# Fused cross-attention and mixture-of-experts layer: later stack loads of the third half, and filler matmuls in front of the first passes

## What is computed

```
x = x + xattn(layernorm(x), ctx)        # x, ctx: 8 x 256 x 512, channels x tokens
    q, k, v = Wq x + bq, Wk c + bk, Wv c + bv      # 16 heads of 16 channels
    p = softmax(q k / sqrt(16));  out = Wo (p v) + bo
x = x + ffn(layernorm(x))               # rows of 512, rmsnorm, router to 8 experts, top 2,
                                        # gated experts 512 -> 256 -> 512, one shared expert
```

## Time and profile before

| | |
|---|---|
| median of 3 runs | 884.27 us (884.0 to 884.33) |
| the profiled execution, its own time | 882.7 us |
| its span in the trace | 880.9 us |
| mean granted TensorE clock over the span | 0.977 of full speed |
| TensorE busy | 827.0 us, 94% |
| VectorE busy | 518.6 us, 59% |
| ScalarE busy | 401.1 us, 46% |
| GpSimd busy | 223.1 us, 25% |
| moved by DMA | 110.45 MB |

### The profile page before, as it was taken

One profiled execution on the slowest core, in us unless ns is written; L12 is line 12 of the kernel. 1 busy time (PEld: TensorE's weight loads), 2 busy tenths in 40 slices (PEclk: granted clock), 3 DMA queues, 4 the chain that ended last, 5 costly groups with the idle time before them and its releaser, 6 DMA issues. The chain is left out here.

```text
span 880.9 us, 11075 instructions
## 1 busy us (share of the span) xinstructions
PE 827.0 (94%) x3641; PEld 376.0 (43%) x3641; DVE 518.6 (59%) x1043; ACT 401.1 (46%) x751; POOL 223.1 (25%) x206
## 2 busy tenths in 40 slices
PE   6889999999999999999999999999999999999991
PEld 2334333334334333343343355443545555555550
DVE  5686788787777777777778755568532222222220
ACT  1104666656667666666676663110323333323220
POOL 4203013213232132132200111000114444444431
PEclk9879999999999999999999999999999999999996
DMA  8876365546546655565551232941625555455542
GB/s 272 187 195 192 88 136 136 134 90 157 127 109 137 148 136 121 103 160 124 115 108 29 84 92 74 389 148 48 249 63 96 90 92 93 90 95 94 95 84 36
DMA packets 47017, 110.45 MB, mean 125 GB/s; under 512 B 11684, under 2 KB 12708, under 8 KB 42724
## 3 DMA queue, kind: packets, MB, share of 16 engines
q1 hardware_dynamic: 35548, 80.23, 36.0%
q0 software_dynamic: 11328, 29.37, 16.2%
q10 hardware_dynamic: 88, 0.16, 0.1%
HBM read 68.44 MB, written 41.16 MB: 124 GB/s over the span
## 5 line engine op out<-in xcount | busy, mean ns | idle before, releaser
L850 DVE TENSOR_REDUCE negmax<-front_ps 128x1 f32<-128x512 f32 x512 | 323.8, 682 | 108.7 <-PE front_ps L702 108.3
L637 ACT ACTIVATE probs<-st_ps 128x512 f32<-128x512 f32 x512 | 280.1, 600 | 187.0 <-PE st_ps L736 186.6
L1289 PE MATMUL big_ps<-w_gu,attn 128*128 x312 | 140.4, 593 | 0.8 <-ACT attn L1138 0.8
L1099 POOL DMA_INDIRECT out<-x_sb,row_i x39 | 61.7, 1583 | 136.0 <-DMA out<-x_sb,row_i 108.5
L736 PE MATMUL st_ps<-stacks 50*128 50x512 f32 x256 | 78.7, 496 | 7.6 <-ACT probs L637 4.4
L1483 DVE TENSOR_TENSOR zeros<-attn,big_ps 128x256 f32<-128x256 f32 x39 | 16.4, 421 | 116.4 <-ACT attn L1157 116.4
L1289 PEld LDWEIGHTS big_ps<-w_gu,attn 128*128 128x128 f32 x312 | 56.2, 190 | 57.0 <-issue 57.0
L736 PE MATMUL st_ps<-q_stack,k_stack 50*128 50x512 f32 x256 | 74.8, 492 | 3.8 <-ACT probs L637 2.7
L702 PE MATMUL front_ps<-stacks 48*128 48x512 f32 x256 | 71.3, 450 | 5.5 <-DMA stacks<-parts_dram 3.0
L374 POOL TENSOR_TENSOR attn<-attn,recip 128x512 f32<-128x512 f32 x15 | 19.2, 1279 | 207.8 <-DMA recip<-rec_dram 207.8
L673 PE MATMUL proj_ps<-early,w_t 128*128 128x512 f32 x128 | 67.2, 647 | 4.7 <-ACT early L590 2.5
(11 more groups left out here) (167 smaller groups left out, 902.0 us busy)
## 6 DMA issues: line engine op xcount, KB each, us to landing
parts_dram<-early SPq DMA_DIRECT2D x32, 512.0 KB, 4.7
stacks<-parts_dram SPq DMA_DIRECT2D x32, 256.0 KB, 5.6
w_gu<-in_gate_up SPq DMA_DIRECT2D x8, 1024.0 KB, 14.4
x_sb<-in_x SPq DMA_DIRECT2D x8, 512.0 KB, 7.4
early<-in_ctx POOLq DMA_DIRECT2D x8, 512.0 KB, 8.2
stacks<-parts_dram SPq DMA_DIRECT2D x32, 128.0 KB, 6.3
k_stack<-parts_dram SPq DMA_DIRECT2D x16, 256.0 KB, 5.0
q_stack<-parts_dram SPq DMA_DIRECT2D x16, 256.0 KB, 5.8
```

Source lines behind the costliest of these rows:

```text
L637: nc.scalar.activation(probs[:, k % 2, u % GH, :], score_bank(UNITS * s + u), ACT.Exp, scale=SCALE).then_inc(exp_done, 1)
L850: nc.vector.tensor_reduce(negmax[:, n % 2, c:c + 1], smax_bank(UNITS * n + u), AX_X, ALU.max, negate=True).then_inc(max_done, 1)
L1099: nc.gpsimd.indirect_dma_start(out_rows, bass.IndirectOffsetOnAxis(ap=row_i[:, k:k + 1], axis=0), y_sb[:, k % RING, :], None, compute_op=A ...
L1289: mm = nc.tensor.matmul(gu_ps[:, :], h_t[:, k % 2, a, :], w_gu[:, bass.ds(expert, 1), a, :], start=(a == 0), stop=(a == DT - 1))
```

## The change

SP puts off the loads of half 2's stacks: the k stack's four transfers go behind the store of the second piece of half 0's maxima rows, the q stack's four behind the loads of that piece. In front of both it waits for `first_loaded`, the arrival of the first piece. `FIRST` is 3, so `FIRST - 1` is half 2. TensorE gets three fillers of 512 columns in front of the first pass of half 0, behind the bias product, and one such filler behind each of the two pairs of first passes of half 1. The definition of `filler` only moves up.

```diff
--- before.py
+++ after.py
@@ -487,9 +487,13 @@
                     for i in range(2):
                         write_part(n, i)
                     for i in range(2):
-                        load_stack(n, i)
+                        if n < FIRST - 1:
+                            load_stack(n, i)
+                sp.wait_ge(first_loaded, 16 * TILES)
                 rows_half_out(sp, 1)
+                load_stack(FIRST - 1, 0)
                 rows_half_in(sp, 1, rows_loaded[0])
+                load_stack(FIRST - 1, 1)
                 load_x(4, B)
                 sp.dma_start(rms_bc[:, :], rms_w.rearrange("(o d) -> o d", o=1).broadcast_to([P, D])).then_inc(shared_loaded, 16)
                 sp.dma_start(w_rt[:, :, :], router_t).then_inc(shared_loaded, 16)
@@ -652,6 +656,10 @@
                 for _ in range(4):
                     nc.tensor.matmul(pv_ps[:, :], zeros[:, 0:P], zeros[:, :], start=True, stop=True)
                 pe.wait_ge(w_loaded, 16)
+
+                def filler(bank):
+
+                    nc.tensor.matmul(bank, zeros[:, 0:P], zeros[:, 0:bank.shape[-1]], start=True, stop=True)
 
                 def project_qk(n, i, kts=range(CT)):
                     s = n - 3
@@ -764,11 +772,9 @@
                         mm = nc.tensor.matmul(st_ps[:, 0, o:o + 1], w_o[:, kt, o * P:(o + 1) * P], bv_col[:, kt:kt + 1],
                                               start=(kt == 0), stop=(kt == CT - 1))
                 mm.then_inc(bo_ready, 1)
+                for _ in range(3):
+                    filler(pv_ps[:, :])
                 pe.wait_ge(ident_ready, 2)
-
-                def filler(bank):
-
-                    nc.tensor.matmul(bank, zeros[:, 0:P], zeros[:, 0:bank.shape[-1]], start=True, stop=True)
 
                 for u in range(0, UNITS, TILES):
                     max_pass(0, u)
```

## The result

The changed kernel takes **878.63 us** (median of 13 runs, 874.64 to 885.42), the kernel before, measured beside it, 884.33 us (13 runs, 880.46 to 888.48). The ratio is 0.9933, with an interval of 0.9904 to 0.9962: by the ratio about 5.9 us faster, where 8.5 were forecast. The forecast of 875.7 is 2.9 us too low; the measured time lies inside the range given. The runs of each kernel spread over 8 to 11 us, so the median alone tells little about parts of 2 us.

The account below looks back on a forecast made before the run. TensorE, busy 94%, was taken as the bound, with gains only where it idles or its clock drops. Leads of 3.69 and 4.84 us sum to 8.53: 874.2 us profiled, 875.7 against the median, range 873.5 to 880.9.

Parts of the forecast that it names:

- Part 1: First passes of half 0: three fillers inside the stack wait keep TensorE's clock at 1.00, lead 3.08 us.
- Part 2: Half 0's maxima rows: with half 2's loads moved, ACT's store takes 1.5 us, and the 2.12 us wait goes.
- Rival B: ACT's first-rows store is slow by itself, 7.6 us whatever SP does; 876.4 us, chance 0.08.
- Part 3: First passes of half 1 with two fillers: first scores at 53.86 against 57.55, lead 3.69 us.
- Part 4: Three steps from half 0's first scores run at full clock instead of half, gaining 4.84 us together.
- Rival A: The clock falls at the hand-over to the scores all the same; only lead 3.69 remains, 880.6 us, chance 0.14.
- C: Rival: the fillers do not hold the clock in the first passes of half 0; 878.8 us, chance 0.03.
- the queue runs empty at about 84.8: SP's transfer queue: half 1's rows stored at 84.8, loaded by 88.3, wanted at 89.2, so 0.9 us of slack.
- the stack loads' 8.7 us at 181 GB/s: Half 2's stack loads, 1.57 MB in SP's queue from 53.6, were taken to end at 62.3.
- The mild case: Queue contention makes half 1's rows 2 to 5 us late, eating lead one for one; 877 to 880 us, chance 0.09.
- The rival's slower end: The 3.95 MB of x and weights move at 181 GB/s, not 335; half 1's rows late, 888.0 us, chance 0.04.
- rival D: Half 1's maxima rows come late, beyond 0.9 us of slack; chance 0.09 for 877 to 880 us, 0.04 for 888.0.

Follow-up runs that it names:

- e8: The changed kernel without the three fillers in front of half 0's first pass; 879.59 us, ratio to the kernel before 0.995.
- e1: The changed kernel without any of the fillers, only the stack loads of half 2 moved; 881.8 us, ratio to the kernel before 0.9976.
- e7: The changed kernel without the two fillers between the first passes of half 1; 879.21 us, ratio to the kernel before 0.9941.
- e3: The changed kernel with all half 2 stack loads issued before the second rows' store and loads; 874.62 us, ratio to the kernel before 0.9911.
- e5: The changed kernel unedited, run and profiled a second time; 879.81 us, ratio to the kernel before 0.9935.
- e4: The changed kernel with the loads of x (batches 4 to 7) and later weights behind half 3's q stack loads; 874.92 us, ratio to the kernel before 0.9893.
- e2: The changed kernel with its five fillers but half 2's stack loads left where they were; 881.48 us, ratio to the kernel before 0.9957.
- e6: e3 with six warm-up matmuls in front of the projections instead of four; 875.48 us, ratio to the kernel before 0.9887.
- e10: e4 unedited, run a second time on another call's chip; 870.09 us, ratio to the kernel before 0.9893.
- e11: The kernel before with six warm-up matmuls instead of four, no other edit; 878.82 us, ratio to the kernel before 0.9994.

## Why the prediction was right, and where not

- **Part 1, front fillers, 3.08 us.** Right: fourth pair at 4.26 us behind the first as against 4.25, and e8 without them loses 3.09. They delayed nothing that shows: in the eight other traces that have them TensorE still waited 0.36 to 1.53 us for the stacks behind them.
- **Part 2, the moved loads.** Right in place and size: the store takes 1.48 us (forecast 1.5), no transfer is waited for at the first scores. Rival B (chance 0.08) is excluded by e1 and by the changed kernel's own rows.
- **Part 3, 3.69 us.** Right in the sum (3.71). The remark that the scores could come 1.0 us sooner at most without the two fillers was wrong for their start, they come 1.93 us sooner (e7). I had counted two maxima as work in front of the scores; they run beside them. But the first step then waits for them, and one step later 0.66 us is left, so as a bound on what could be gained the 1.0 held.
- **Part 4, 4.84 us.** Right: the three steps took 3.00, 3.85 and 2.94 us, forecast 2.93, 3.86 and 2.94, and the lead at their end was 8.49. Rival A (the clock falls at the hand-over, 0.14) did not come: 1.00 in every trace that has the fillers and the move. Nor did C.
- **The step that failed: "the queue runs empty at about 84.8", with 0.9 us of slack for half 1's rows.** I gave the case in which this goes wrong 0.09 and the undisturbed one 0.62; it was in both traces of the changed kernel. The term that was mis-sized is the stack loads' 8.7 us at 181 GB/s. In the trace the engines moved 152, 164 and 142 GB/s in the three windows of 4 us from 60 to 72 us, before the faster x loads (386 and more) took over: 12.2 us from the first stack load on. Why the rate was lower than the 181 is open. The rest up to half 3's k stack took 14.2 us, forecast 15.0. So from the first of these loads to that k stack it took 26.4 us, forecast 23.7 (53.6 to 77.3). From there to the landed rows it was 11.8 us, forecast 11.0 (77.3 to 88.3). These 2.7 and 0.8 us use up the 0.9 of slack and leave a wait of 2.6; measured were 2.27 and 2.45.
- **The price of the late rows was read too low.** The mild case was costed "one for one". But behind a wait of 2.3 us the clock fell: two steps took 7.85 us in the changed kernel and 5.77 in e3 (89.50 to 95.27), 2.1 us more. The full bill was 4.4 us of the 8.5 in the profiled execution, and 5.6 in e5 (third step of half 1 at 71.67, in e4 at 66.11). I had added the clock only to the case that ended slower than before, although the 2.12 us in front of the first scores had shown that a wait of this length can cost it.
- The rival's slower end (everything at the stack loads' rate) did not come: x and the weights moved at 386 to 405 GB/s, faster than the 335 I had used, which gave back 0.8 us of the loss.
- The median of 878.63 lies 2.9 us over the forecast, in large part, as it seems, since the runs mix: with late rows and without (874.64 to 876 are the undisturbed ones by the comparison with e4; that single runs of the changed kernel had no wait is argued from their times, since only two were traced). The last stretch of the kernel, which alone differs by up to 3.8 us between the traces, adds to the spread. That the median lies inside the range given is no support for the 0.9 us of slack: the range was wide enough to hold the mild case of rival D, 877 to 880, and that is the case that came.
- **The fall around 541 us**, for which I had allowed 2 us either way, came in seven traces (before, e1, e2, e5, e6, e7, e10) and not in the other six. It shows no clear price: from the first product of the expert part to the end the traces of before, changed and e1 to e8 take 339.2 to 342.9 us with it and 339.1 to 340.4 without.

## What to carry to other kernels

A gain in one stage moves every later demand forward, but not the transfers behind a full queue: before counting on the lead at the end, compute for each shared queue when it runs empty and when the next small transfer in it is wanted, and take the slack with the worst rate seen, since less than 1 us of slack is none. A wait of TensorE can cost more than its length: the waits of 2.27, 2.45 and 2.60 us for half 1's rows cost the wait and a stretch at half clock behind it, about twice their length together. That is no rule, since waits of 2.21 to 2.69 us in front of the first projections (before, e1, e3) left the clock at 1.00. Bulk loads that are wanted late belong behind the small transfers that are wanted soon, even if the queue stands empty when they could be issued.

## What the runs showed of the hardware that was not expected

- A small transfer on one engine's queue is held up by bulk loads on another's. ACT's 16 KB store took 1.5 us beside an empty SP queue, 3.9 us when it was issued 0.2 us behind the first of SP's stack loads (e2) and 7.6 us when it was issued 4.3 us behind it, and its two loads of 8 KB took 7.0 us behind all eight (e2). The Trainium skill (DMA: Bandwidth & Descriptors, "Queues, rings and completion order") has the transfer engines take turns between queues packet by packet. These rows show no sign that turns help a small transfer: SP's own store, issued 4.7 us behind the first of the same loads, took 7.3 us in e3 and 8.4 in e6, about as long as ACT's 7.6.
- The granted clock stayed at 1.00 behind waits of 0.92 (e7), 1.08 (e8) and 1.53 us (e5, in front of the first pass) and fell behind waits of 1.88 (e2), 2.27, 2.45 (e5) and 2.60 us (e6). The lengths do not sort the cases: it also fell some 2 us behind a wait of 1.26 us (e11), and behind short standstills for VectorE, 0.61 us the longest that is listed (e7), while it stayed at 1.00 behind waits of 2.21 (before), 2.44 (e3) and 2.69 us (e1) in front of the first projections. What stood in front of each wait differs, so this is an observation, not a threshold.
- The same instructions at the start take 6 us more in one execution than in another (first pass at 35.20 against 28.3 to 30.0 in all others), where the context let the projections start at 10.54 instead of about 9 us, 3.0 us behind the last warm-up matmul, and they then ran at half clock.
